# Contexts of two heads in one quadrant of the PSUM, and the second values behind the next batch's first scores

## The reference

```
x = _layernorm(x + _L0_attn_ref(...))          # self attention, then attention to two past states
x = _layernorm(x + _L0_xattn_ref(x, ctx_1024, ctx_1024, ...))   # cross attention
x = _layernorm(x + _L0_ffn_ref(...))           # 16 experts, top 2
x = _layernorm(x + _L1_attn_ref(...)) ; x = _layernorm(x + _L1_xattn_ref(...)) ; x = _layernorm(x + _L1_ffn_ref(...))

def _L0_attn_ref(hidden_states, past_states, ...):
    q, k, v = heads of hidden_states @ W + b            # 16 heads of 8
    ctx = softmax(q k^T / sqrt(8)) v                    # per batch: 16 heads, 128 x 128
    output = merge(ctx) @ Wo + bo
    rq = heads of output @ Wrq + brq
    rk, rv = heads of past_states @ Wrk/Wrv + b         # 2 past states of 256 tokens
    rctx = softmax(rq rk^T / sqrt(8)) rv                # per past state
    recursive_output = merge(rctx).mean over the two
    gate = sigmoid([output, recursive_output] @ Wg + bg)
    return output * (1 - gate) + recursive_output * gate
```

## Time and profile before

| | us |
|---|---|
| median of 3 runs | 634.48 (633.09 to 636.98) |
| the profiled execution: time | 634.75 |
| the profiled execution: span of the core | 633.0 |
| TensorE busy | 537.8 (85%) |
| VectorE busy | 460.0 (73%) |
| ScalarE busy | 344.3 (54%) |
| GpSimd busy | 216.0 (34%) |

### The profile page before, as it was taken

The page is one execution under the profiler, slowest core; times in us unless marked ns, Lnnn a source line. Parts: engine busy times, 40 slices in busy tenths (PEclk is TensorE's granted clock), DMA queues, the critical chain, the costliest instruction groups (busy, mean ns, idle before and its releaser), DMA issues.

```text
span 633.0 us, 14406 instructions
## 1 busy us (share of the span) xinstructions
PE 537.8 (85%) x5354; PEld 296.8 (47%) x5354; DVE 460.0 (73%) x1049; ACT 344.3 (54%) x588; POOL 216.0 (34%) x349
## 2 busy tenths in 40 slices
PE   2587888699999999999998788877999986979784
PEld 0254554223333333333334555654434465879673
DVE  4465666778899998998954577755678645977786
ACT  2165566347787778778766466551100153417761
POOL 6113211701111322340233333252442275676542
PEclk9999999769999999999999799999999998979999
DMA  5448541030001011010101033014556700001001
GB/s 151 112 113 216 150 131 37 3 101 2 2 3 52 4 49 52 3 51 14 41 2 52 19 102 90 17 47 166 182 185 226 268 17 1 2 9 42 2 18 51
DMA packets 44546, 44.08 MB, mean 70 GB/s; under 512 B 6903, under 2 KB 35319, under 8 KB 44343
## 3 DMA queue, kind: packets, MB, share of 16 engines
q1 hardware_dynamic: 42460, 42.01, 22.6%
q10 hardware_dynamic: 2016, 1.15, 0.7%
HBM read 25.18 MB, written 1.18 MB: 42 GB/s over the span
## 4 chain that ended last, share of the span: by engine, by line
PE 56%; DVE 14%; ACT 11%; issue 7%; DMA 6%; POOL 4%; ACTq 1%; SPq 1%; DVEq 0%; POOLq 0%
PE banks L1143 11%; PE banks L1123 7%; ACT probs L685 5%; PE banks L1737 5%; PE banks L1062 4%; PE banks L448 4%; PE banks L538 4%; PE banks L1154 3%; DVE rec_negmax L1372 3%; DMA past_mem<-gates 2%; PE banks L521 2%; DMA shared<-neg_T 1%; DVE negmax L827 1%; DVE left L398 1%; PE banks L496 1%
## 5 line engine op out<-in xcount | busy, mean ns | idle before, releaser
L1372 DVE TENSOR_REDUCE rec_negmax<-banks 128x2 bf16<-128x512 f32 x256 | 168.3, 688 | 26.0 <-PE banks L1062 20.6
L1265 ACT ACTIVATE probs<-banks 128x1024 f32<-128x1024 f32 x128 | 131.0, 1026 | 50.6 <-PE banks L1123 50.0
L827 DVE TENSOR_REDUCE negmax<-banks 128x8 bf16<-128x1024 f32 x64 | 78.2, 1222 | 50.3 <-PE banks L496 50.3
L1062 PE MATMUL banks<-shared 62*128 62x512 bf16 x256 | 98.2, 401 | 3.5 <-DVE rec_negmax L1372 3.5
L1123 PE MATMUL banks<-shared 64*128 64x256 bf16 x512 | 98.2, 280 | 1.6 <-DMA shared<-rec_neg_T 1.6
L1143 PE MATMUL banks<-probs,past_mem 128*32 128x256 f32 x1024 | 83.8, 399 | 2.0 <-ACT o_T L1272 2.0
L685 ACT ACTIVATE probs<-banks 128x1024 f32<-128x1024 f32 x64 | 65.5, 1024 | 29.9 <-PE banks L521 29.7
L1737 PE MATMUL banks<-shared,w_r 128*128 128x512 f32 x128 | 60.2, 605 | 6.4 <-DVE shared L1851 6.4
L1123 PEld LDWEIGHTS banks<-shared 64*128 64x128 bf16 x512 | 30.1, 94 | 74.6 <-issue 68.4
L1851 DVE TENSOR_TENSOR shared<-past_mem,out_T 128x512 f32<-128x512 f32 x64 | 42.7, 693 | 15.6 <-DMA past_mem<-gates 14.6
L1479 POOL TENSOR_TENSOR rctx<-o 128x64 f32<-128x64 f32 x32 | 10.2, 318 | 125.5 <-DVE o L1393 125.4
(11 more groups left out here) (248 smaller groups left out, 1016.7 us busy)
## 6 DMA issues: line engine op xcount, KB each, us to landing
...
shared<-rec_neg_T SPq DMA_DIRECT2D x64, 2.0 KB
...
```

What stands on the lines that cost most here:

```text
L827: nc.vector.tensor_reduce(c.negmax[:, i % 2, :].rearrange("p (r j) -> p r j", r=2)[:, :, 4 * half:4 * half + 4], c.max_pair.rearrange("p ( ...
L1062: self.nc.tensor.matmul(c.max_banks[r], c.QT[64 * r:64 * r + 62, g % 2, j, off:off + P], c.rKT[64 * r:64 * r + 62, j, :], start=True, stop ...
L1265: nc.scalar.activation(c.probs[:, i % 4, :], c.score_pairs[i % 2], ACT.Exp, scale=HEAD_SCALE)\
L1372: self.nc.vector.tensor_reduce(out, c.max_banks[r].rearrange("p (a t) -> p a t", a=NP_PAST), AX_X, ALU.max, negate=True).then_inc(s["rec_m ...
```

## The change

Two things are changed.

First, two heads share a quadrant. A head's 8 values and its one now stand at columns 16 to 24 of its 32, the rest are zeros, and all heads' columns form one row of 512. The weights of an odd head are its own 32 columns, so its context comes out in partitions 16 to 24 of the quadrant; those of an even head start 16 columns later and end in the zeros of the next head, so its context comes out in partitions 0 to 8. Both are accumulated in the same quadrant and columns. The 16 heads of a batch fill 256 columns: copied and transposed are two pieces in place of four. In past attention eight heads fill the bank, so copy, transposes, division and sum come after eight steps: 2 of each for a pair in place of 4, the division and the sum on twice the elements. The order of the heads in the projections' rows (`by_row`) follows, and the memsets of the value tiles cover them whole.

Second, in self and cross attention the second values of a batch and ScalarE's copy of its contexts move into the next slot. TensorE's slot is now: scores(t-2, first), values(t-3, second), max_scores(t, first), scores(t-2, second), turn_ctx(t-3), cross_out(t-4), values(t-2, first), max_scores(t, second), turn_norm(t-3), project_v(t), window(t), turn_max(t). ScalarE's: exp(first), copy_ctx(t-3), copy_neg, rows, window(t-1), exp(second), copy_norm. In the last slot of self attention the values and the copy of its last batch stay where they were. In past attention GpSimd's mix stands before the sum of the first heads.

```diff
@@ -210,6 +211,8 @@
     c.past_mem = sb("past_mem", [P, n_rq + n_rv])
     c.rq_parts = c.past_mem[:, 0:n_rq].bitcast(BF16).rearrange("p (g n t) -> p g n t", g=4, n=3)
     c.rV = c.past_mem[:, n_rq:].rearrange("p (t h v) -> p t h v", t=2 * NP_PAST, h=NH)
+    c.V_rows = c.V.rearrange("p i h v -> p i (h v)")
+    c.rV_rows = c.rV.rearrange("p t h v -> p t (h v)")
     c.gate_rows = c.past_mem[:, 0:SPREAD * GROUP].rearrange("p (q t) -> p q t", q=SPREAD)
     c.moe_T = c.past_mem[:, SPREAD * GROUP:(SPREAD + 1) * GROUP]
     c.scaled = c.rKT_words.rearrange("p (q t) -> p q t", q=RING)
@@ -231,7 +234,7 @@
 
     c.rec_negmax = sb("rec_negmax", [P, 2, 4, 2, 8], BF16)
     c.rec_neg_T = sb("rec_neg_T", [8, 4, PAIR], BF16)
-    c.o8 = sb("o8", [P, 2, 2, P // 4])
+    c.o8 = sb("o8", [P, 2, 2, P // 2])
     c.rctx = sb("rctx", [P, 2, P])
     c.rec_T = sb("rec_T", [P, PAIR])
     c.gate_t = sb("gate_t", [P, PAIR])
...
@@ -349,6 +352,17 @@
 K_ORDER = (0, 1, 2, 0, 1, 0)
 
 
+def head_rows(h):
+
+    first = h * HV + (0 if h % 2 else HO)
+    return slice(first, first + HV)
+
+
+def packed(bank):
+
+    return bank[:, 0:NH * HO].rearrange("p (h v) -> p h v", v=HO)
+
+
 def column(x):
 
     return x.rearrange("p a d -> p (a d)")
...
@@ -529,15 +543,15 @@
             if i:
                 pe.wait_ge(*s.after(ph + "ctx", i))
             elif cross:
-                pe.wait_ge(*s.after("rec_ctx", 4 * NPAIR))
+                pe.wait_ge(*s.after("rec_ctx", 2 * NPAIR))
             else:
                 pe.wait_ge(*s.after("set_memset", 7))
-        for h in range(8 * half, 8 * half + 8):
-            j, r, q = h // 2, h % 2, h % 4
-            col = (r * 4 + j % 4) * P
-            last = nc.tensor.matmul(c.ctx_bank[HV * q:HV * (q + 1), h // 4 * P:(h // 4 + 1) * P],
-                                    c.V[:, i % 4, h, :], c.probs[:, (2 * i + half) % 4, col:col + P],
-                                    start=True, stop=True)
+        for a in range(2):
+            for q in range(4):
+                col = (q % 2 * 4 + 2 * a + q // 2) * P
+                last = nc.tensor.matmul(c.ctx_bank[HV * q:HV * (q + 1), half * P:(half + 1) * P],
+                                        c.V_rows[:, i % 4, head_rows(8 * half + 2 * q + a)],
+                                        c.probs[:, (2 * i + half) % 4, col:col + P], start=(a == 0), stop=(a == 1))
         last.then_inc(s[ph + "pv"], 1)
 
     def turn_ctx(i):
@@ -546,7 +560,7 @@
             pe.wait_ge(*s.after(ph + "v", i + 3))
         else:
             pe.wait_ge(*s.after(ph + "norm", i))
-        for g in range(4):
+        for g in range(2):
             last = nc.tensor.transpose(c.misc[:, g * P:(g + 1) * P], c.o_T[:, i % 2, g * P:(g + 1) * P],
                                        c.ident_f[:, :])
         last.then_inc(s[ph + "o_turned"], 1)
...
@@ -628,6 +642,8 @@
     def slot(t):
         if 0 <= t - 2 < B:
             scores(t - 2, 0)
+        if 0 <= t - 3 < B:
+            values(t - 3, 1)
         if t < B:
             max_scores(t, 0)
         elif lead:
@@ -636,13 +652,14 @@
             tail(t, 0)
         if cross and t == 4:
             turn_x(2, ("rec_y", NPAIR))
+        if 0 <= t - 2 < B:
+            scores(t - 2, 1)
         if 0 <= t - 3 < B:
             turn_ctx(t - 3)
         if cross and 0 <= t - 4 < B:
             cross_out(t - 4)
         if 0 <= t - 2 < B:
             values(t - 2, 0)
-            scores(t - 2, 1)
         if t < B:
             max_scores(t, 1)
         elif lead:
@@ -654,7 +671,7 @@
         if t < B:
             project_v(t)
         window(t)
-        if 0 <= t - 2 < B:
+        if not cross and t == SELF_SLOTS - 1:
             values(t - 2, 1)
         if t < B:
             turn_max(t)
@@ -689,7 +706,7 @@
         act.wait_ge(*s.after(ph + "pv", 2 * i + 2))
         if i >= 2:
             act.wait_ge(*s.after(ph + "o_turned", i - 1))
-        nc.scalar.copy(c.o_T[:, i % 2, :], c.ctx_bank).then_inc(s[ph + "ctx"], 1)
+        nc.scalar.copy(c.o_T[:, i % 2, 0:PAIR], c.ctx_bank[:, 0:PAIR]).then_inc(s[ph + "ctx"], 1)
 
     def copy_norm(i):
         g, gp, at_ = group_of(i)
@@ -760,6 +777,8 @@
     def slot(t):
         if 0 <= t - 2 < B:
             exp(t - 2, 0)
+        if 0 <= t - 3 < B:
+            copy_ctx(t - 3)
         if tail:
             tail(t, 0)
         if cross and t == 4:
@@ -803,7 +822,9 @@
         dve.wait_ge(*s.after(ph + "v_proj", i + 1))
         if i >= 4:
             dve.wait_ge(*s.after(ph + "pv", 2 * i - 6))
-        nc.vector.tensor_tensor(c.V[:, i % 4, :, 0:HD], c.v_cols.rearrange("p (h d) -> p h d", h=NH),
+        elif i == 0 and not cross:
+            dve.wait_ge(*s.after("set_memset", 7))
+        nc.vector.tensor_tensor(c.V[:, i % 4, :, HO:HO + HD], c.v_cols.rearrange("p (h d) -> p h d", h=NH),
                                 b_v[:, :].rearrange("p (h d) -> p h d", h=NH), ALU.add).then_inc(s[ph + "v"], 1)
 
     def halves():
...
@@ -1136,28 +1157,28 @@
         if i == 0:
             pe.wait_ge(*s.after("past_v", 1))
             pe.wait_ge(*s.after("self_ctx", B))
-        elif t == 0:
-            pe.wait_ge(*s.after("rec_ctx", 4 * n + g))
+        elif t == 0 and g % 2 == 0:
+            pe.wait_ge(*s.after("rec_ctx", 2 * n + g // 2))
         for q in range(4):
             col = (q % 2) * 512 + (q // 2) * PAIR
             last = self.nc.tensor.matmul(c.ctx_bank[HV * q:HV * (q + 1), past * PAIR:(past + 1) * PAIR],
-                                         c.rV[:, t, 4 * g + q, :], c.probs[:, i % 4, col:col + PAIR],
-                                         start=(half == 0), stop=(half == 1))
+                                         c.rV_rows[:, t, head_rows(8 * (g // 2) + 2 * q + g % 2)], c.probs[:, i % 4, col:col + PAIR],
+                                         start=(t == 0 and g % 2 == 0), stop=(t == 3 and g % 2 == 1))
         last.then_inc(s["rec_pv"], 1)
 
     def turn_ctx(self, n, g):
         c, pe, s = self.c, self.pe, self.s
-        pe.wait_ge(*s.after("rec_ctx", 4 * n + g + 1))
-        self.claim("rec_norm", 4 * n + g + 1)
+        pe.wait_ge(*s.after("rec_ctx", 2 * n + g + 1))
+        self.claim("rec_norm", 2 * n + g + 1)
         for v in range(2):
             for past in range(2):
                 last = self.nc.tensor.transpose(self.bank[:, (2 * v + past) * P:(2 * v + past + 1) * P],
-                                                c.o_T[:, g, past * PAIR + v * P:past * PAIR + (v + 1) * P], c.ident_f[:, :])
...
@@ -1230,13 +1251,13 @@
                 if i == 1:
                     self.turn_max(0, 1)
                 if k == 2 and n:
-                    self.turn_ctx(n - 1, 3)
+                    self.turn_ctx(n - 1, 1)
                 if k in (3, 7):
                     self.turn_max(n, k // 4 + 2)
                 if k == 5 and n:
                     self.turn_sum(n - 1)
-                if k in (6, 10, 14):
-                    self.turn_ctx(n, k // 4 - 1)
+                if k == 10:
+                    self.turn_ctx(n, 0)
                 if k == 9 and n:
                     self.gate_product(n - 1)
                 if k in (11, 15) and n + 1 < NPAIR:
@@ -1249,9 +1270,9 @@
         self.values(NPAIR - 1, STEPS - 2)
 
 
-def last_bank(c, n, g=3):
-
-    return c.proj_bank if (n, g) == (NPAIR - 1, 3) else c.misc
+def last_bank(c, n, g=1):
+
+    return c.proj_bank if (n, g) == (NPAIR - 1, 1) else c.misc
 
 
 def past_attention_act(c, act):
@@ -1266,10 +1287,10 @@
             .then_inc(s["rec_exp"], 1)
 
     def copy_ctx(n, g):
-        act.wait_ge(*s.after("rec_pv", STEPS * n + 4 * g + 4))
+        act.wait_ge(*s.after("rec_pv", STEPS * n + 8 * g + 8))
         if n:
-            act.wait_ge(*s.after("rec_o_turned", 4 * n + g - 3))
-        nc.scalar.copy(c.o_T[:, g, :], c.ctx_bank).then_inc(s["rec_ctx"], 1)
+            act.wait_ge(*s.after("rec_o_turned", 2 * n + g - 1))
+        nc.scalar.copy(c.o_T[:, 2 + g, :], c.ctx_bank).then_inc(s["rec_ctx"], 1)
 
     def copy_neg(n, q):
         act.wait_ge(*s.after("rec_max_turned", 4 * n + q + 1))
...
@@ -1384,14 +1405,15 @@
 
     def normalise(self, n, g):
         c, dve, nc, s = self.c, self.dve, self.nc, self.s
-        dve.wait_ge(*s.after("rec_o_turned", n * 4 + (g + 1)))
-        turned = last_bank(c, n, g).rearrange("p (q v) -> p q v", v=HV)
-        nc.vector.reciprocal(c.recip[:, 0, :], turned[:, :, HD]).then_inc(s["rec_recip"], 1)
-        dve.wait_ge(*s.after("rec_recip", n * 4 + (g + 1)))
+        dve.wait_ge(*s.after("rec_o_turned", 2 * n + g + 1))
+        turned = last_bank(c, n, g).rearrange("p (q v) -> p q v", v=HO)
+        recip = c.recip[:, :, :].rearrange("p a b -> p (a b)")
+        nc.vector.reciprocal(recip, turned[:, :, HD]).then_inc(s["rec_recip"], 1)
+        dve.wait_ge(*s.after("rec_recip", 2 * n + g + 1))
         if g > 0 or n:
-            dve.wait_ge(*s.after("rec_ctx_sum", n * 4 + g))
+            dve.wait_ge(*s.after("rec_ctx_sum", 2 * n + g))
```

(26 more changed lines are left out.)

30 lines of the change are left out of this document (16 added, 14 removed), and 4 rows, old and new, of the table each.

## The result

The changed kernel's median is 631.9 us (626.2 to 637.4, 20 runs) against 636.4 for the kernel before in its 20 runs (631.9 to 639.8): a ratio of 0.993 [0.990, 0.996]. Forecast were 621.0, with 612 to 630 as the range. The sign is right, a third of the gain is there.

What follows compares the result with a forecast made beforehand. TensorE was taken to bound past attention, VectorE close behind; self and cross slots were chains of waits. Savings of 8.5 + 2.2 + 2.6 + 0.5 = 13.8 us off 634.75 gave 621.0 us, range 612 to 630.

Steps and rivals of the forecast that it cites:

- past attention: Stage where TensorE sets the pace: 16 fewer transpose groups save 9.4 us, 8.5 taken after allowing for VectorE.
- self slots: Self attention, slots 2 to 17: gains where a projection runs, small losses elsewhere, 2.2 us less in sum.
- cross slots: Cross attention: plain slots, slots with projections and the head gain, slots 6 and 10 lose; 2.6 us less in sum.
- experts' start and the rest: Behind slot 17: first experts' matmuls no longer wait behind the last second values; 0 to 1.5 us, 0.5 taken.
- Rival (a): Past attention: VectorE and TensorE lock step and slots come out even; 3 to 5 us off, 630; chance 0.14.
- VectorE idling under 20 us: Sign of a right forecast in past attention: VectorE's idle time before its maxima falls below 20 us, from 26.0.
- the projection slots: Six self slots with high part, rest and next projection: values' 0.46 off TensorE's path, 5.31 us each, 2.0 gained.
- Slots 3 and 13 lose 0.1 each: Self attention slots without a projection: each gets 0.1 us longer because the second maximum starts later.
- A plain slot: Self slot without a projection: 4.45 us instead of 4.36, with VectorE's second maximum from 2.60.
- rival (c): TensorE's clock: one more 1.2 GHz stretch gives 628, chance 0.07; one less gives 614, chance 0.04.
- Slots 7 and 12: Self slots where the row maxima's DMA ends last: issued 0.27 us later, 0.5 us lost together.
- Rival (d): Row maxima's DMA becomes the last wait in nearly all self and cross slots: slower, 670 us; chance 0.03.

Runs made afterwards that it cites:

- second execution: Another profiled execution of the unaltered changed kernel, taken because the earlier profiled one was among the slow ones: 627.7 us, span 625.9.
- the move alone: The kernel before with only the new order of slots, one head in a quadrant and four transposes kept: 646.8 us, ratio 1.018.
- the early second scores alone: Changed kernel with slots in the old order, except second scores directly behind the first maxima's matmuls: 632.6 us, ratio 0.996 to the kernel before.
- first execution: The changed kernel's original profiled execution, the slowest of its 20 runs: 637.4 us, span 635.6.
- `filled`: Changed kernel with value-projection products repeated in five TensorE waits of self attention, outputs the same: 629.3 us, ratio 0.989 to the kernel before.
- packing alone: Changed kernel with slots in the old order, keeping only two heads in a quadrant: 628.0 us, ratio 0.987 to the kernel before.

## Why the prediction was wrong

Worked out were 13.8 us less. The second execution of the changed kernel has 7.1 less in its span, 0.2 of it ahead of the first exponential, and by stage:

| term | forecast | measured |
|---|---|---|
| past attention | -8.5 | -7.5 |
| self slots | -2.2 | +0.4 |
| cross slots | -2.6 | -3.0 |
| experts' start and the rest | -0.5 | +3.2 |

The last two rows belong together, since 1.9 us of the last slots only moved behind the last exponential: forecast -3.1, measured +0.2.

**The step that failed is the price of the second part of the change.** The prediction took the move as a gain in the slots and at the experts' start. In the runs the move alone makes the kernel 1.8% slower (646.8 us), the early second scores alone take 0.9% from the packing's gain, and in the changed kernel self attention came to +0.4 for a forecast of -2.2 and all behind past attention to +0.2 for -3.1. The terms, one by one:

**Past attention: 0.7 to 1.0 too much.** TensorE's price was right: a group of four transposes still takes 0.59 us to the next start. VectorE was mis-sized: the reciprocal of 32 elements took 349 ns and not 265, the multiply 425 and not 414, together 12.4 us in place of 10.9. Rival (a) came in part. Its sign was VectorE named ahead of TensorE's maxima matmuls in sum over 8 us; the two rows of this wait have 22.3 us after, but had 14.0 before, so the mark was already passed. Its price, 3 to 5 us off in all, did not come in this stage. "VectorE idling under 20 us" was wrong: it is 25.6.

**Self slots.** In the projection slots the working held to 0.01 us, 52.46 - 47.14 = 5.32 where 5.31 was said, save in slot 6 with 5.54. The six have gained 1.7 us for 2.0. Its words for that gain were that "the values' 0.46 of TensorE is gone" from the path; in the slots without a projection these values were what TensorE did while VectorE took its maxima, and the early second scores now wait for ScalarE and hold up the products for the second maximum. "Slots 3 and 13 lose 0.1 each" was the term that was mis-sized: at a clock of 1.00 slot 13 takes 5.19 for 4.51 and slot 3 takes 4.66 for 4.36. A plain slot was forecast at 4.45 with the second maximum at 2.60, which starts at 2.78; and the forecast compared with 4.36, where packing by itself gives 4.22. A group of two transposes takes 48.92 - 48.55 = 0.37 us to the next start, so two less are 0.22 and not 0.30. The Trainium skill ("TensorEngine Tiling (Array Packing)", Key Properties) says that a change of the tiling mode drains TensorE; the row agrees in direction, for two transposes cost more than half of four.

**The clock, rival (c).** Its mechanism was named, "Less TensorE work in slots with the same chain", and one more stretch was given 0.07. The first execution has three more in self attention alone (from 34, 65 and 95 us), the second has one (28 to 38 us). How much an execution pays differs: granted clock and time go loosely together in the 20 runs (0.956: 627.1; 0.929 to 0.932: 632.3 to 637.4), and the kernel spreads over 11 us where the one before spread over 8. The Trainium skill ("TensorE: Matmul & The Clock Gate", Part 1) has the clock gated by how busy TensorE has been; the profiled execution of `filled` agrees, with 1.00 from 20 to 96 us; the median over all its executions, 0.947, does not show it. What part of the loss the clock is stays open.

**Slots 7 and 12** were forecast 0.5 longer together, as if the DMA took the same time from its own issue. Slot 7 lost 0.18. In slot 12 it was the load of Y that set the landing, and the load moved with the slot, from 2.4 us ahead of the maxima's DMA to 1.4 in the second execution and 0.65 in the first. The second execution has 6.85 for 5.78, 1.07 lost, and packing alone 6.83. Rival (d), this wait in nearly all slots, did not come.

**Cross slots: too much.** To the first exponentials of slot 16, where the cut-off plays no part, packing alone gains 2.4 us and the changed kernel 1.1: the move took 1.3 back. Plain slots came to 4.88 for 4.85, slots 5 and 9 to 5.33, slots 6 and 10 to 5.33 as forecast; slot 7 took 5.99 and 6.08 in a stretch at 0.50, where `filled` has 4.89. The largest single gain is in slot 4, 10.25 before and 8.51 after. The prediction had the second scores gain there, but packing alone, without them, has 8.85, and the execution before had a low clock for 6.8 us around it, where this one has 3.4.

**Experts' start.** "Behind slot 17 the first experts' matmuls no longer stand behind the last batch's second values" brought no gain: from the first exponentials of cross slot 16 to the last expert matmul pass 88.5 us before, 89.3 in the second execution, 89.4 and 87.1 with the old order packed. What moves the rest of the kernel from 202.5 to 211 between executions stays open, and with it a part of the missing gain.
